# A two-layer cross-attention program: the first weights asked for on two DMA queues, context parts and router weights asked for one stage earlier

## The reference, cut to what matters

```
x = x + L0_xattn(layernorm(x), context)    # Wq, Wk, Wv each plus a low-rank down @ up * alpha/32; 16 heads of 64; + 4 last tokens
x = x + L0_attn(layernorm(x))              # a state-space block
x = x + L0_ffn(layernorm(x))               # 8 experts; logits = xn @ gate_w.T, best 1
x = x + L1_xattn(layernorm(x), context)    # K = l2norm(context @ Wk + bk), V = context @ Wv + bv, 16 heads of 16
x = x + L1_attn(layernorm(x))              # self attention with rope
x = x + L1_ffn(layernorm(x))               # 8 experts; logits = xn @ gate_w.T, best 2 of logits + beta; one shared expert
```

## Time and profile before

| what | us |
|---|---|
| median of three runs | 2032.73 |
| the profiled execution, its own time | 2033.02 |
| its span, first to last instruction | 2031.3 |
| PE busy (90% of the span) | 1827.0 |
| ACT busy | 1026.5 |
| DVE busy | 994.8 |
| POOL busy | 668.9 |
| mean granted TensorE clock, as a share of 2.4 GHz | 0.941 |

### The profile page before, as it was taken

One profiled execution on the slowest core, in us unless ns is written; L12 is line 12 of the kernel. 1 busy time (PEld: TensorE's weight loads), 2 busy tenths in 40 slices (PEclk: granted clock), 3 DMA queues, 4 the chain that ended last, 5 costly groups with the idle time before them and its releaser, 6 DMA issues. The chain is left out here.

```text
span 2031.3 us, 32604 instructions
## 1 busy us (share of the span) xinstructions
PE 1827.0 (90%) x13272; PEld 1281.4 (63%) x13272; DVE 994.8 (49%) x1502; ACT 1026.5 (51%) x1395; POOL 668.9 (33%) x331
## 2 busy tenths in 40 slices
PE   6889999999899999999999765958998899666999
PEld 2567777777677777777767444447445644344887
DVE  3566566665665757566650444246002400374665
ACT  1245555555555555555531322026997699434443
POOL 2007566565555757566573131012000100110000
PEclk9899999999999999999998787879999899877999
DMA  5450000000303000000030200023564455200220
GB/s 184 135 188 6 6 17 1 16 7 6 99 1 120 27 6 17 6 14 4 1 83 1 62 1 0 19 78 100 88 104 116 92 92 98 84 2 20 86 98 26
DMA packets 80804, 107.38 MB, mean 53 GB/s; under 512 B 22088, under 2 KB 63792, under 8 KB 76560
## 3 DMA queue, kind: packets, MB, share of 16 engines
q1 hardware_dynamic: 79616, 104.24, 19.4%
q10 hardware_dynamic: 1040, 1.05, 0.2%
HBM read 62.77 MB, written 21.50 MB: 41 GB/s over the span
## 5 line engine op out<-in xcount | busy, mean ns | idle before, releaser
L762 POOL TENSOR_TENSOR sums<-sums,probs 128x1024 f32<-128x1024 f32 x224 | 532.7, 2378 | 332.8 <-ACT probs L797 316.2
L861 DVE TENSOR_REDUCE part_max<-psum_banks 128x2 f32<-128x1024 f32 (+1 forms) x256 | 312.8, 1225 | 130.1 <-PE psum_banks L1035 128.2
L797 ACT ACTIVATE probs<-psum_banks 128x1024 f32<-128x1024 f32 x240 | 233.6, 1022 | 112.5 <-PE psum_banks L1082 112.0
L852 DVE TENSOR_TENSOR keys<-psum_banks,keys 64x512 fp32r<-64x512 f32 x256 | 176.3, 689 | 185.4 <-ACT keys L775 181.2
L2446 ACT ACTIVATE probs<-psum_banks,k_inv_norm 128x1024 f32<-128x1024 f32 x256 | 258.0, 1259 | 2.1 <-PE psum_banks L2461 2.0
L1096 PE MATMUL psum_banks<-probs,values 128*64 128x256 f32 x2048 | 249.9, 386 | 0.0
L775 ACT ACTIVATE keys<-psum_banks 64x512 fp32r<-64x512 f32 x256 | 151.8, 593 | 172.3 <-PE psum_banks L1010 168.6
L1096 PEld LDWEIGHTS psum_banks<-probs,values 128*64 128x64 f32 x2048 | 136.1, 137 | 86.5 <-issue 30.1
L780 ACT ACTIVATE values<-psum_banks 128x512 f32<-128x512 f32 x128 | 76.6, 599 | 200.8 <-PE psum_banks L1022 200.8
L2473 PE MATMUL psum_banks<-probs,values 128*32 128x256 f32 x2048 | 166.0, 396 | 2.9 <-ACT probs L2446 2.9
L1064 PEld LDWEIGHTS psum_banks<-q_hi,keys 128*128 128x128 f32 x1024 | 141.4, 192 | 12.8 <-issue 1.5
(11 more groups left out here) (438 smaller groups left out, 2934.2 us busy)
## 6 DMA issues: line engine op xcount, KB each, us to landing
k_pairs<-keys SPq DMA_DIRECT2D x192, 128.0 KB, 4.1
wk_pair<-wkv_parts SPq DMA_DIRECT2D x16, 256.0 KB, 2.9
wv_quad<-wkv_parts SPq DMA_DIRECT2D x8, 512.0 KB, 3.9
ctx_parts<-cA_hi SPq DMA_DIRECT2D x2, 2048.0 KB, 11.7
ctx_parts<-cA_lo SPq DMA_DIRECT2D x2, 2048.0 KB, 13.3
ctx_parts<-cB SPq DMA_DIRECT2D x2, 2048.0 KB, 17.6
c1A_hi<-ctx_parts SPq DMA_DIRECT2D x16, 256.0 KB, 4.2
c1A_lo<-ctx_parts SPq DMA_DIRECT2D x16, 256.0 KB, 4.5
```

What stands on the lines that cost most here:

```text
L762: pool.tensor_tensor(sums[:, :, :, :], probs[:, 0, :, :, :] if step == 1 else sums[:, :, :, :], probs[:, step % SLOTS, :, :, :], ALU.add). ...
L797: act.activation(probs[:, step % SLOTS, :, :, :], scores, ACT.Exp, scale=SCALE0).then_inc(p_ready, 1)
L852: dve.tensor_tensor(keys[rows(1 - h), m % 2, h, columns_of(c)], psum[rows(h), bank, :], keys[rows(h), m % 2, h, columns_of(c)].bitcast(F32 ...
L861: dve.tensor_reduce(part_max[:, :, i, c], psum[:, bank:bank + 2, 0:width], AX, ALU.max).then_inc(m_read, 1)
```

## The change

1. The 20 weight transfers are split. SP asks for x and the seven large ones (k, v, q, with a semaphore for each letter); ACT, in the same block, asks for the 13 small ones on a semaphore of their own. In `l0_weights` PE and DVE wait first for the small ones only; DVE waits for the large ones of a letter before the first of its four sums.
2. `router_weights` holds the router's buffers and semaphore outside `route`; its `start` is given to `layernorm_transposed` as `meanwhile`, in both layers.
3. The context parts get a buffer at a fixed address that lives through the L1 cross attention, with three slots in place of four and semaphores for each batch. The first three chunks of batch 0 are asked for in the second block of `l1x_queries`; those of batch 1 in `l1x_attention` of batch 0, behind the key pairs of n = 1.
4. In `l1x_keys_values` SP loads chunks 3 to 7 only, each behind the values of chunk c-3, and issues the first key pairs behind chunk 6 in place of chunk 5.
5. The ring `probs` has three slots in place of four; ACT's step waits until `weigh(step - 3)` is done.

```diff
--- before.py
+++ after.py
@@ -92,8 +92,12 @@
                              core.args["x"].rearrange("b (t p) d -> p (b t) d", p=P)).then_inc(x_in, 16)
-                meanwhile(sp)
+                start_large(sp)
                 sp.wait_ge(x_in, 16)
+            @block.scalar
+            def _(act):
+                start_small(act)
@@ -187,23 +191,30 @@
     raw, down = s.raw, s.down
-    pairs = []
+    small, large = [], {}
...
         d, w = a[f"L0_xattn_{n}_down"], a[f"L0_xattn_W{n}"]
-        pairs += [(down[:, 2 * i, :], d[0:P, :]), (down[0:CB, 2 * i + 1, :], d[P:CD, :]), (down[CB:P, 2 * i + 1, :], d[P:CD, :]),
-                  (raw[n][:, 0, :], w[0:P, :]), (raw[n][0:CB, 1, :], w[P:CD, :]), (raw[n][CB:P, 1, :], w[P:CD, :])]
-    pairs += [(down[:, 4:6, :], a["L0_xattn_q_down"].rearrange("(c p) n -> p c n", p=P)),
-              (s.wq[:, :, :], a["L0_xattn_Wq"].rearrange("(c p) n -> p c n", p=P))]
-    pairs += [(s.up[n][:, :], a[f"L0_xattn_{n}_up"]) for n in "kvq"]
-    pairs += [(s.alpha[:, i:i + 1], broadcast_rows(a[f"L0_xattn_{n}_alpha"], P)) for i, n in enumerate("kvq")]
-    arrived = core.sem(ctx, "w_qkv_arrived")
-    s.loads = [(arrived, 16 * len(pairs))]
-    def start(sp):
-        for dst, src in pairs:
-            sp.dma_start(dst, src).then_inc(arrived, 16)
-    s.start = start
+        small += [(down[:, 2 * i, :], d[0:P, :]), (down[0:CB, 2 * i + 1, :], d[P:CD, :]), (down[CB:P, 2 * i + 1, :], d[P:CD, :])]
+        large[n] = [(raw[n][:, 0, :], w[0:P, :]), (raw[n][0:CB, 1, :], w[P:CD, :]), (raw[n][CB:P, 1, :], w[P:CD, :])]
+    small += [(down[:, 4:6, :], a["L0_xattn_q_down"].rearrange("(c p) n -> p c n", p=P))]
+    small += [(s.up[n][:, :], a[f"L0_xattn_{n}_up"]) for n in "kvq"]
+    small += [(s.alpha[:, i:i + 1], broadcast_rows(a[f"L0_xattn_{n}_alpha"], P)) for i, n in enumerate("kvq")]
+    large["q"] = [(s.wq[:, :, :], a["L0_xattn_Wq"].rearrange("(c p) n -> p c n", p=P))]
+    small_in = core.sem(ctx, "w_small_arrived")
+    large_in = {n: core.sem(ctx, f"w_{n}_arrived") for n in "kvq"}
+    s.small_in = small_in, 16 * len(small)
+    s.large_in = {n: (large_in[n], 16 * len(large[n])) for n in "kvq"}
+    def start_small(act):
+        for dst, src in small:
+            act.dma_start(dst, src).then_inc(small_in, 16)
+    def start_large(sp):
+        for n in "kvq":
+            for dst, src in large[n]:
+                sp.dma_start(dst, src).then_inc(large_in[n], 16)
+    s.start_small, s.start_large = start_small, start_large
@@ -231,8 +242,7 @@
             def _(pe):
-                for semaphore, count in s.loads:
-                    pe.wait_ge(semaphore, count)
+                pe.wait_ge(*s.small_in)
@@ -246,8 +256,7 @@
             def _(dve):
-                for semaphore, count in s.loads:
-                    dve.wait_ge(semaphore, count)
+                dve.wait_ge(*s.small_in)
@@ -257,6 +266,8 @@
                     w = (wq if n == "q" else raw[n])[:, c, half * 512:(half + 1) * 512]
+                    if j % 4 == 0:
+                        dve.wait_ge(*s.large_in[n])
@@ -1218,7 +1229,7 @@
             last = l0_last_tokens(core, early)
-            setup(core, w_qkv.start)
+            setup(core, w_qkv.start_large, w_qkv.start_small)
@@ -1669,14 +1680,30 @@
-def route(core, xnT, gate_w, beta, top, weight, tag):
+def router_weights(core, ctx, gate_w, beta, tag):
+    s = Tiles()
+    s.gate = core.sbuf(ctx, tag + "_gate", [EX, D])
+    s.bias = core.sbuf(ctx, tag + "_beta", [P, EX])
+    s.arrived = core.sem(ctx, tag + "_gate_in")
+    s.loads = 16 if beta is None else 32
+    def start(sp):
+        sp.dma_start(s.gate[:, :], gate_w).then_inc(s.arrived, 16)
+        if beta is not None:
+            sp.dma_start(s.bias[:, :], broadcast_rows(beta, P)).then_inc(s.arrived, 16)
+    s.start = start
+    return s
+def route(core, xnT, w, beta, top, weight, tag):
...
     with ExitStack() as ctx:
-        gate = core.sbuf(ctx, tag + "_gate", [EX, D])
+        gate, bias, gate_in, loads = w.gate, w.bias, w.arrived, w.loads
         gateT = core.sbuf(ctx, tag + "_gateT", [P, DC, EX])
-        bias = core.sbuf(ctx, tag + "_beta", [P, EX])
@@ -1697,14 +1723,7 @@
         picked = core.sem(ctx, tag + "_picked")
-        loads = 16 if beta is None else 32
         with nc.Block() as block:
-            @block.sync
-            def _(sp):
-                sp.dma_start(gate[:, :], gate_w).then_inc(gate_in, 16)
-                if beta is not None:
-                    sp.dma_start(bias[:, :], broadcast_rows(beta, P)).then_inc(gate_in, 16)
@@ -1953,8 +1973,9 @@
         weight = core.sbuf(ctx, "route1", [P, TT, EX])
-        layernorm_transposed(core, xnT, "moe1")
-        route(core, xnT, a["L1_ffn_gate_w"], a["L1_ffn_beta"], 2, weight, "moe1")
+        w_router = router_weights(core, ctx, a["L1_ffn_gate_w"], a["L1_ffn_beta"], "moe1")
+        layernorm_transposed(core, xnT, "moe1", w_router.start)
+        route(core, xnT, w_router, a["L1_ffn_beta"], 2, weight, "moe1")
@@ -2148,6 +2169,8 @@
             def _(sp):
+                for c in range(C_SLOTS):
+                    load_context_parts(sp, core, 0, s.c, c)
@@ -2235,21 +2258,38 @@
+C_SLOTS = 3
+C_PARTS_AT = 210912
+def context_part_buffers(core, ctx):
+    c = Tiles()
+    c.parts = core.nc.alloc_sbuf_tensor_at(core.unused("c1_parts"), [P, 3, C_SLOTS, CHUNK], F32R, offset=C_PARTS_AT)
+    c.arrived = [[core.sem(ctx, f"c1_arrived{i}_b{b}") for i in range(C_SLOTS)] for b in range(B)]
+    return c
+def load_context_parts(sp, core, b, c, n):
+    for i in range(3):
+        sp.dma_start(c.parts[:, i, n % C_SLOTS, :].bitcast(F32),
+                     core.context_parts[b, i, :, n * CHUNK:(n + 1) * CHUNK]).then_inc(c.arrived[b][n % C_SLOTS], 16)
...
     G = 4
-    SLOTS = 4
+    SLOTS = C_SLOTS
+    cA_hi, cA_lo, cB = (s.c.parts[:, i, :, :] for i in range(3))
+    arrived = s.c.arrived[b]
     with ExitStack() as ctx:
-        cA_hi = core.sbuf(ctx, "c1A_hi", [P, SLOTS, CHUNK], F32R)
-        cA_lo = core.sbuf(ctx, "c1A_lo", [P, SLOTS, CHUNK], F32R)
-        cB = core.sbuf(ctx, "c1B", [P, SLOTS, CHUNK], F32R)
...
         sem = lambda n: core.sem(ctx, n)
-        arrived = [sem(f"c1_arrived{i}") for i in range(SLOTS)]
@@ -2275,13 +2315,10 @@
             def _(sp):
-                for c in range(CHUNKS):
-                    if c >= SLOTS:
-                        sp.wait_ge(v_done, 2 * (c - SLOTS + 1))
-                    for i, part in enumerate((cA_hi, cA_lo, cB)):
-                        sp.dma_start(part[:, c % SLOTS, :].bitcast(F32),
-                                     core.context_parts[b, i, :, c * CHUNK:(c + 1) * CHUNK]).then_inc(arrived[c % SLOTS], 16)
-                    if c == SLOTS + 1:
+                for c in range(SLOTS, CHUNKS):
+                    sp.wait_ge(v_done, 2 * (c - SLOTS + 1))
+                    load_context_parts(sp, core, b, s.c, c)
+                    if c == CHUNKS // 2 + 2:
@@ -2415,7 +2452,8 @@
     with ExitStack() as ctx:
-        probs = core.sbuf(ctx, "probs1", [P, 4, GROUP, L])
+        PROB_SLOTS = 3
+        probs = core.sbuf(ctx, "probs1", [P, PROB_SLOTS, GROUP, L])
@@ -2428,6 +2466,9 @@
                     load_key_pairs(sp, s, keys, n // 2, n % 2, k_ready)
+                    if n == 1 and b + 1 < B:
+                        for c in range(C_SLOTS):
+                            load_context_parts(sp, core, b + 1, s.c, c)
@@ -2440,10 +2481,10 @@
                     act.wait_ge(s_done, step + 1)
-                    if step >= 4:
-                        act.wait_ge(pv_done, step - 3)
+                    if step >= PROB_SLOTS:
+                        act.wait_ge(pv_done, step - PROB_SLOTS + 1)
                     bank = 2 + 2 * (step % 3)
-                    act.activation(probs[:, step % 4, :, :], psum[:, bank:bank + 2, :].rearrange("p t (a q) -> p (t a) q", q=L),
+                    act.activation(probs[:, step % PROB_SLOTS, :, :], psum[:, bank:bank + 2, :].rearrange("p t (a q) -> p (t a) q", q=L),
@@ -2471,7 +2512,7 @@
                         last = pe.matmul(psum[32 * r:32 * r + 32, g % 2, 0:L], s.values_flat[:, at:at + 32],
-                                         probs[:, step % 4, r % 2 * 2 + r // 2, :], start=kt == 0, stop=kt == KT - 1,
+                                         probs[:, step % PROB_SLOTS, r % 2 * 2 + r // 2, :], start=kt == 0, stop=kt == KT - 1,
@@ -2598,6 +2639,7 @@
                (s.wo[:, :, :], a["L1_xattn_Wo"].rearrange("(c p) n -> p c n", p=P))]
+    s.c = context_part_buffers(core, ctx)
```

More of the change, by code:

```diff
@@ L81, in broadcast_rows, with setup @@
     return ap.rearrange("(a n) -> a n", a=1).to_broadcast([n, ap.shape[0]])
-def setup(core, meanwhile):
+def setup(core, start_large, start_small):
     nc = core.nc
@@ L1688, in route @@
         chosen = core.sbuf(ctx, tag + "_chosen", [P, top, TT, EX])
-        gate_in = core.sem(ctx, tag + "_gate_in")
         numbered = core.sem(ctx, tag + "_numbered")
@@ L1822, in l0_mixture @@
```

(5 more changed lines are left out.)

## The result

The changed kernel takes 2004.55 us (median of 6 runs, 1999.98 to 2006.38) against 2033.25 (6 runs, 2026.19 to 2039.87): a ratio of 0.9848, with a 95% interval from 0.9834 to 0.9863, so 1.4 to 1.7% faster. The forecast was 2000.5, in a range from 1994 to 2009. The profiled execution took 2004.96 us, its span 2003.2 against 2031.3, so 28.1 us are to be found in the trace.

What follows compares the result with a forecast made beforehand. PE was taken as the bound, busy for 90% of the span, with gains only where it stands still. 5.0 + 4.3 + 9.8 + 13.4 = 32.5 us off 2033.0 gave 2000.5, range 1994 to 2009.

Steps and rivals of the forecast that it cites:

- Part 1: Start: split issuing lets the weights' stage start earlier than 19.96; 5.0 us taken, upper end 5.5, lower 2.1 or nothing.
- rival A: Start: small weights end among the large ones, or ACT issues slowly; gain 2.1 us, time 2003.4; chance 0.25.
- Part 2: Both routers: PE no longer waits for their weights at the block's start; 1.4 and 2.9 us, 4.3 together.
- Part 3: L1 keys and values, batch 0: waits for chunks 0 and 6 go; 56.2 us becomes 46.4, a gain of 9.8.
- The 0.3 us for chunk 7: L1 keys and values, each batch: wait for chunk 7's transfer behind the key pairs; 0.3 us, bounds 0 and 2.5.
- Part 4: L1 keys and values, batch 1: waits go, chunk 0 takes 5.58; 58.4 us becomes 45.0, a gain of 13.4.
- Part 5: Context ring and ACT's ring in attention, both of three: the added waits cost nothing.
- B: Keys and values: chunk 7 takes chunk 6's place, 2.5 us late per batch, clock falls; 10.3 us, 2010.8; chance 0.12.
- C: Keys and values: something other than the transfers holds the stages; under half of the sum, 2020 to 2026; chance 0.04.
- D: Attention: the ring of three stops ACT, 0.65 us more in each of 256 steps, 166 us slower, 2166; chance 0.02.
- some 3: Rest of the program: shifted times can move the clock's falls and rises, some 3 us either way.
- the low end: 1994: waits for chunk 7 at zero, batch 0's chunk 0 at the high clock (1.4), 3 us of clock elsewhere.

Runs made afterwards that it cites:

- experiment 2: Changed kernel with SP asking at the start only for x and k's large parts, v's and q's once the small ones are in; 2001.48 us.
- Experiment 9: Changed kernel with the routers' weights asked for in the routers' own blocks, as before, in both layers; 2012.95 us against 2005.07.
- experiment 5: Changed kernel with the 12 key pair transfers put back behind chunk 5's context parts instead of chunk 6's; 2014.62 us.
- experiment 6: Kernel before with only the 12 key pair transfers moved behind chunk 6's context parts instead of chunk 5's; 2023.17 us against 2034.71.
- experiment 7: Changed kernel without the load ahead of batch 1's first three context chunks, which the block asks for itself; 2010.59 us.
- Experiment 8: Kernel before with only the ring of probabilities in L1's attention cut from four tiles to three; 2033.87 us against 2034.71.

## Why the prediction was right, and where it was not

**Part 1: the step that failed** is "I take 5.0, near the upper end". It measured 2.1, the lower end, as rival A had it: "the last small one lands with the last byte of all, near 17.9", and it was 17.8. The issuing went as forecast (13 issues, 0.57 each, layernorm at 8.75 against 8.5). What I read wrong was the share. I gave ACT's queue 85 GB/s from one pair of 1 MB transfers and took the 13 small ones by their bytes. But what a small transfer waited for here was what was in flight on the engines that it lands on: 0.5 KB took 8.0 us before (11.92 to 19.96), 10.0 in the changed kernel, 3.4 behind k's parts alone (experiment 2). Bytes didn't set it. The saturation of the earlier trace rows and the rule that the prediction quotes from the Trainium skill (DMA: Bandwidth & Descriptors, "Issuing engines are not separate DMA queues") stood on the same side, and I chose against both.

**Part 2** was right for the waits (4.2 of 4.3) and short by 2.7: what lies behind a wait at the low clock was costed for the chunks, and not for the router. Experiment 9 put it back, wait and clock, 7.9 us in whole runs.

**Part 3** gave 10.0 for 9.8. The last chunk starts 40.61 us after its block's (POOL's first instruction, 1357.36); 40.8 was forecast. The 0.3 us for chunk 7 was 0 in this profile, chunk 0 took 6.27 for 6.96, chunk 1 5.94 for 5.58, the later ones 5.61, the border 0.35 for 0.06. That chunk 6 hides, and that the order of SP's list does it, experiments 5 and 6 show each from its own side.

**Part 4** gave 13.6 for 13.4, with chunk 0 at the high clock as forecast (5.12 us); experiment 7 shows that it is the load ahead that keeps it there. The 9.85 us for chunk 6 that the sum took away belong to one profile. Experiment 8 has 7.21 in its place and a longer chunk 0 (7.23 for 6.22); counted from that profile, the two stages would have gained 9.8 and 12.8.

**Part 5** cost nothing (experiment 8 for the ring of the probabilities). The context's ring of three was not tried by itself; in the changed kernel chunk 7's load goes out 0.07 us behind the last key pair (1391.52 to 1391.59), so that the key pairs held it and not the ring.

**Rivals.** A held, in part 1 and by its own price of 2003.4 us. B didn't: chunk 7 waited 0.8 us at most, in batch 0, and never 2.5. Its clock term came again as it was: experiment 5 has 4.5 and 1.6 us for the low clock behind a chunk 6 that waits, where B took 4.3 and 1.6; but experiment 8 has 1.7 and 1.6, so which of the two comes is open. C and D didn't come.

**The sum** came out at 32.6 in the stages for 32.5 by luck: two errors cancel, 2.9 too much in part 1 and 2.7 too little behind the router. What parts the 2000.5 from the profiled 2005.0 is the clock in untouched stages, 4.5 us, forecast as "some 3". Between two profiles of the changed kernel alone the spans differ by 5.8 us (2003.2 and 1997.4), and that one stretch by 6.2. One sum of the recorded text is off: the terms that it names for the low end, 0.6, 1.4 and 3 us, give 1995.5 and not 1994.

## What to carry to other kernels

A second issuing queue saved sequencer time here (the layernorm began 4.1 us earlier), but the small transfers still ended among the large. When the small transfers are wanted first, hold the large ones back, and put their issues into a block that has time for them, since a block lasts as long as its longest list, SP's included. Look at what stands between two loads in one engine's list: moving 12 issues by one place was worth 11.5 us. A wait costs its length and what PE then does at the low clock, which was 1.6 to 4.5 us behind waits of 3 to 4, 2.7 behind the first router's of 1.4, and 0.2 behind the second router's of 2.9. The length of the wait doesn't give this price; it has to be read in the trace behind each wait.

## What the runs showed that I had not expected

A wait of 1.4 us in front of the first router's small turns cost another 2.7 us in the mixture behind it, where the clock came back later (0.64 against 0.80 in the stretch above), in all four kernels that had it and in none of the nine other profiles.

One stretch that no edit touches took from 89.6 to 98.9 us, with granted clocks between 0.70 and 0.96 in its middle, and 91.2 and 97.4 in one and the same kernel. What picks the length is open; no run tells it. A gain of 2 to 5 us in this kernel has to be read in the stages of the trace, or over ten runs a side.
